# A GRU with eight experts: the experts' and the candidate's products as quarters of 32 stationary columns, and the low half of y on GpSimd

## What is computed

```python
# x [16, 256, 512], h0 = cond_2048 [16, 512]
def cell(h, x):
    gi = x @ W_ih + b_ih                  # [16, 1536]
    gh = h @ W_hh + b_hh
    i_r, i_z, i_n = jnp.split(gi, 3, axis=-1)
    h_r, h_z, h_n = jnp.split(gh, 3, axis=-1)
    r = sigmoid(i_r + h_r); z = sigmoid(i_z + h_z)
    n = tanh(i_n + r * h_n)
    h_new = (1.0 - z) * n + z * h
    return (h_new, h_new)
hs = swapaxes(scan(cell, h0, swapaxes(x, 0, 1)), 0, 1)          # [16, 256, 512]
s = hs.reshape(-1, 512)
logits = s / max(norm(s), 1e-12) @ router_w                     # 8 experts
rw, selected = top_k(softmax(logits), 2); rw = rw / sum(rw)
out = 0
for e in range(8):
    out = out + combine[:, e, None] * (s @ Wa[e] @ Wb[e])       # 512 -> 128 -> 512
return x + out
```

## Time and profile before

| what | value |
|---|---|
| median of 3 runs | 1091.35 us (1091.34 to 1095.48) |
| the profiled execution's own time | 1092.62 us |
| its span, first to last instruction | 1090.7 us |
| mean granted clock of TensorE | 0.995 of full speed |
| busy: PE, DVE, ACT, POOL | 96%, 83%, 60%, 15% of the span |
| matmuls, weight loads | 28880, 28880 |
| chain that ended last, by engine | PE 88%, DVE 6%, ACT 2%, DMA 2% |

### The profile page before, as it was taken

The page is one execution under the profiler, slowest core; times in us unless marked ns, Lnnn a source line. Parts: engine busy times, 40 slices in busy tenths (PEclk is TensorE's granted clock), DMA queues, the critical chain, the costliest instruction groups (busy, mean ns, idle before and its releaser), DMA issues.

```text
span 1090.7 us, 66722 instructions
## 1 busy us (share of the span) xinstructions
PE 1042.4 (96%) x28880; PEld 846.9 (78%) x28880; DVE 907.2 (83%) x3475; ACT 657.6 (60%) x2445; POOL 163.9 (15%) x419
## 2 busy tenths in 40 slices
PE   2679999999999999999999999999999999999996
PEld 2567788888888888888888888888888888888874
DVE  5689888888888888888888888888888888888885
ACT  4576666666665666566666666566666666665552
POOL 3011211111111111111111111111111111110111
PEclk9899999999999999999999999999999999999999
DMA  9801011111101121101112110101111110110000
GB/s 235 202 14 23 24 33 21 26 34 33 32 24 25 22 33 32 33 24 33 23 23 33 33 33 23 30 18 32 34 32 28 28 23 23 33 24 14 14 14 21
DMA packets 48037, 39.23 MB, mean 36 GB/s; under 512 B 33296, under 2 KB 37504, under 8 KB 47744
## 3 DMA queue, kind: packets, MB, share of 16 engines
q1 hardware_dynamic: 47168, 31.81, 13.3%
q10 hardware_dynamic: 576, 3.15, 0.9%
HBM read 18.95 MB, written 8.39 MB: 25 GB/s over the span
## 4 chain that ended last, share of the span: by engine, by line
PE 88%; DVE 6%; ACT 2%; DMA 2%; issue 1%; SPq 1%; POOL 0%; POOLq 0%; DVEq 0%; ACTq 0%
PE ybank L904 17%; PE pairs L819 15%; PE obank L923 14%; PE gates L851 10%; PE gates L856 10%; PE nbank L837 7%; PE zbank L862 5%; PE zbank L866 5%; PE pairs L812 3%; DMA whh<-in_L_cond_W_hh 2%; PE nbank L880 1%; PE nbank L886 1%; DVE tr L692 1%; DVE acc L744 1%; SPq L315 1%
## 5 line engine op out<-in xcount | busy, mean ns | idle before, releaser
L819 PE MATMUL pairs<-wx,xs 128*32 128x256 f16 x6144 | 214.8, 275 | 0.0
L904 PE MATMUL ybank<-hparts,wa 128*128 128x128 f16 x3000 | 210.7, 220 | 2.8 <-DVE y L732 1.9
L819 PEld LDWEIGHTS pairs<-wx,xs 128*32 128x32 f16 x6144 | 153.2, 97 | 61.5 <-issue 50.9
L923 PE MATMUL obank<-wb,y 128*128 128x512 f16 x741 | 200.2, 379 | 0.3 <-DVE acc L744 0.3
L524 ACT ACTIVATE rr<-pre 128x64 f32<-128x64 f32 x256 | 65.7, 256 | 217.8 <-DVE pre L695 217.8
L904 PEld LDWEIGHTS ybank<-hparts,wa 128*128 128x128 f16 x3000 | 168.3, 98 | 30.4 <-DVE y L732 3.7
L851 PE MATMUL gates<-whh,st 128*32 128x256 f16 x4096 | 157.2, 274 | 16.5 <-DVE st L718 12.7
L856 PE MATMUL gates<-whh,hparts 128*32 128x256 f16 x4096 | 157.0, 273 | 0.0
L692 DVE STREAM_TRANSPOSE tr<-gates 128x256 f32<-128x256 f32 x256 | 115.1, 449 | 43.3 <-PE gates L856 30.5
L744 DVE SCALAR_TENSOR_TENSOR acc<-obank,comb,acc 128x512 f32<-128x512 f32 x186 | 138.5, 744 | 1.5 <-PE obank L923 1.5
L837 PE MATMUL nbank<-xs,win 128*128 128x128 f16 x1512 | 126.1, 220 | 2.8 <-ACT gi_n L514 2.8
(11 more groups left out here) (122 smaller groups left out, 1558.8 us busy)
## 6 DMA issues: line engine op xcount, KB each, us to landing
xin<-in_x SPq DMA_DIRECT2D x32, 256.0 KB
out<-outb SPq DMA_DIRECT2D x32, 256.0 KB
wih<-in_L_cond_W_ih ACTq DMA_DIRECT2D x4, 768.0 KB, 9.2
whh<-in_L_cond_W_hh SPq DMA_DIRECT2D x16, 192.0 KB, 13.1
wih<-in_L_ffn_Wb SPq DMA_DIRECT2D x1, 2048.0 KB, 12.4
wih<-in_L_ffn_Wa SPq DMA_DIRECT2D x8, 128.0 KB, 8.2
whh<-in_L_ffn_Wa SPq DMA_DIRECT2D x8, 128.0 KB, 6.3
xs<-xh SPq DMA_TRANSPOSE x58, 2.5
```

The source lines that it names most:

```text
L819: mm = nc.tensor.matmul(bank[32 * j:32 * j + 32, P:3 * P], turned(b, k, ph)[:, t0:t0 + 2 * B], wx[:, pw, k, j, :], start=False, stop=(k == ...
L904: mm = nc.tensor.matmul(y_at(m)[:, 0:P], wa[:, pw, k, e, :], hparts[:, f % HB, k, :, ph * B:(ph + 1) * B], start=(n == 0), stop=(n == 3 * ...
L923: mm = nc.tensor.matmul(o_at(m)[:, :], y[:, m % 2, ph, :], wb[:, pw, m % NE, :], start=(n == 0), stop=(n == 2))
```

## The change

Three products are written as quarters. For each j = 0 to 3 the columns 32j to 32j + 32 of the stationary operand (`wa`, `win` or `y`) are multiplied by the same moving columns as before, and the output goes to partitions 32j to 32j + 32 of the same bank. One matmul becomes four, one weight load four: 12 become 48 in `expert_down`, 6 become 24 in half of `n_part`, 3 become 12 in `expert_up`. `route` keeps its 128 stationary columns.

VectorE's `split_y` is taken out. ScalarE's `split_y` has a second activation that copies `ybank` as float32 into a new tile `y32`, and GpSimd's new `low_y(m)` subtracts the high part of `y` from it. `expert_down` waits for `yhi_ready` and `y32_ready` in place of `ylo_ready`; `expert_up` still waits for `ylo_ready`.

GpSimd's list is interleaved by steps: `split_x` goes in two halves (s = 7 and s = 0 of the next block), `add_squares` in two pieces (`fold_squares` at s = 1, `add_squares` at s = 2), each held until step n's `both_parts_ready`, and each ahead of that step's `low_y`.

```diff
@@ gpsimd
+            def split_x(b, half, n):
+                of = slice(half * D // 2, (half + 1) * D // 2)
                 pool.wait_ge(xhi_ready, b + 1)
                 pool.wait_ge(x_scaled, b - 2)
+                pool.wait_ge(both_parts_ready, 2 * (n + 2))
+                low = nc.gpsimd.tensor_tensor(xh[:, b % 2, 1, of], x128[:, of], xh[:, b % 2, 0, of], ALU.subtract)
...
+            def low_y(m):
+                pool.wait_ge(yhi_ready, m + 1)
+                pool.wait_ge(y32_ready, m + 1)
+                wait(pool, o_done, m - 1)
+                nc.gpsimd.tensor_tensor(y[:, m % 2, 1, :], y32[:, :], y[:, m % 2, 0, :], ALU.subtract
+                                        ).then_inc(ylo_ready, 1)
...
+            def beside(n):
+                i, s = n // S, n % S
+                if s == 1 and 1 <= i:
+                    fold_squares(i - 1, n)
+                if s == 2 and 1 <= i:
+                    add_squares(i - 1, n)
+                if s == X_AT + 1 and i + 3 < NB:
+                    split_x(i + 3, 0, n)
+                if s == 0 and 1 <= i and i + 2 < NB:
+                    split_x(i + 2, 1, n)
+                if 0 <= n - DOWN:
+                    low_y(n - DOWN)
+                if s == 3 and 1 <= i:
+                    invert_norm(i - 1)
+                    gaps(i - 1)
+                if s == 4 and 1 <= i:
+                    combine(i - 1)
@@ scalar, split_y
                 nc.scalar.activation(y[:, m % 2, 0, :], y_at(m)[:, 0:P], ACT.Copy, scale=1 / PART_SCALE
                                      ).then_inc(yhi_ready, 1)
+
+                wait(act, ylo_ready, m)
+                nc.scalar.activation(y32[:, :], y_at(m)[:, 0:P], ACT.Copy, scale=1 / PART_SCALE).then_inc(y32_ready, 1)
@@ vector
-            def split_y(m):
-                dve.wait_ge(yhi_ready, m + 1)
-                nc.vector.scalar_tensor_tensor(out=y[:, m % 2, 1, :], in0=y_at(m)[:, 0:P], scalar=1 / PART_SCALE,
-                                               in1=y[:, m % 2, 0, :], op0=ALU.mult, op1=ALU.subtract
-                                               ).then_inc(ylo_ready, 1)
@@ tensor, n_part
-                    mm = nc.tensor.matmul(n_at(b, m)[:, 0:P], win[:, pw, k, m, :], turned(b, k, ph),
-                                          start=(i == 0), stop=(i == 11), skip_group_check=True)
+                    for j in range(K):
+                        own = slice(32 * j, 32 * j + 32)
+                        mm = nc.tensor.matmul(n_at(b, m)[own, 0:P], win[:, pw, k, m, own], turned(b, k, ph),
+                                              start=(i == 0), stop=(i == 11), skip_group_check=True)
@@ tensor, expert_down
-                wait(pe, ylo_ready, m if m <= LAST else m - 1)
+                wait(pe, yhi_ready, m if m <= LAST else m - 1)
+                wait(pe, y32_ready, m if m <= LAST else m - 1)
...
-                        mm = nc.tensor.matmul(y_at(m)[:, 0:P], wa[:, pw, k, e, :],
-                                              hparts[:, f % HB, k, :, ph * B:(ph + 1) * B],
-                                              start=(n == 0), stop=(n == 3 * K - 1))
+                        for j in range(K):
+                            own = slice(32 * j, 32 * j + 32)
+                            mm = nc.tensor.matmul(y_at(m)[own, 0:P], wa[:, pw, k, e, own],
+                                                  hparts[:, f % HB, k, :, ph * B:(ph + 1) * B],
+                                                  start=(n == 0), stop=(n == 3 * K - 1), skip_group_check=True)
@@ tensor, expert_up
-                    mm = nc.tensor.matmul(o_at(m)[:, :], y[:, m % 2, ph, :], wb[:, pw, m % NE, :],
-                                          start=(n == 0), stop=(n == 2))
+                    for j in range(K):
+                        own = slice(32 * j, 32 * j + 32)
+                        mm = nc.tensor.matmul(o_at(m)[own, :], y[:, m % 2, ph, own], wb[:, pw, m % NE, :],
+                                              start=(n == 0), stop=(n == 2), skip_group_check=True)
```

More of the change, by code:

```diff
@@ L135, in gru_moe_kernel @@
         comb = sb("comb", [P, NE])
+        y32 = sb("y32", [P, P])
         y = sb("y", [P, 2, 2, P], F16)
@@ L220, in gru_moe_kernel @@
         yhi_ready = sem("yhi_ready")
+        y32_ready = sem("y32_ready")
         ylo_ready = sem("ylo_ready")
@@ L395, in split_win, with fold_squares, add_squares @@
                                         ).then_inc(win_split, 1)
-            def split_x(b):
+            def split_x(b, half, n):
+                of = slice(half * D // 2, (half + 1) * D // 2)
                 pool.wait_ge(xhi_ready, b + 1)
                 pool.wait_ge(x_scaled, b - 2)
[L401 to L405, removed]
+                pool.wait_ge(both_parts_ready, 2 * (n + 2))
+                low = nc.gpsimd.tensor_tensor(xh[:, b % 2, 1, of], x128[:, of], xh[:, b % 2, 0, of], ALU.subtract)
+                if half:
+                    low.then_inc(xlo_ready, 1)
+            def fold_squares(f, n):
                 pool.wait_ge(sq_ready, f + 1)
-                if f + 1 < NB:
-                    pool.wait_ge(both_parts_ready, 2 * ((f + 1) * S + 3))
+                if n < T:
+                    pool.wait_ge(both_parts_ready, 2 * (n + 2))
                 nc.gpsimd.tensor_tensor(sq2[:, :], sq[:, 0:2 * P], sq[:, 2 * P:4 * P], ALU.add).then_inc(sq_step, 1)
+            def add_squares(f, n):
                 pool.wait_ge(sq_step, f * SQ_STEPS + 1)
                 wait(pool, logits_done, f)
+                if n < T:
+                    pool.wait_ge(both_parts_ready, 2 * (n + 2))
                 nc.gpsimd.tensor_tensor(sqs[:, :], sq2[:, 0:P], sq2[:, P:2 * P], ALU.add).then_inc(sq_step, 1)
+            def low_y(m):
[4 more added lines that the diff above has]
+                                        ).then_inc(ylo_ready, 1)
             def invert_norm(f):
@@ L447, in _, with last_experts @@
                 split_win(k)
[L448 to L456, removed]
+            def beside(n):
[15 more added lines that the diff above has]
+                    combine(i - 1)
+            def last_experts():
+                fold_squares(NB - 1, T)
+                add_squares(NB - 1, T)
+                for m in range(LAST, T):
+                    low_y(m)
+                    if m == LAST + 3:
+                        invert_norm(NB - 1)
+                        gaps(NB - 1)
+                    if m == LAST + 4:
+                        combine(NB - 1)
+            for n in range(T):
+                beside(n)
+            last_experts()
         @block.scalar
@@ L752, in beside @@
                     add_expert(n - ADD)
-                if 0 <= n - DOWN < T:
-                    split_y(n - DOWN)
                 if s == 3 and 1 <= i <= NB:
@@ L763, in last_experts @@
                 for m in range(LAST, T):
-                    split_y(m)
                     add_expert(m - 1)
```

## The result

The changed kernel takes 1411.65 us (median of 4 runs, 1406.27 to 1416.30) against 1092.02 (median of 4, 1091.34 to 1095.48). The ratio is 1.292, with a 95% interval of 1.286 to 1.297. The prediction was 1052, in a range of 1046 to 1076: wrong in sign, by 360 us. The profiled execution took 1410.65 us, with a span of 1408.4 and a mean granted clock of 0.994, so TensorE's clock is the same as before.

What follows compares the result with a forecast made beforehand. TensorE, busy 96% of the span, was taken as the bound. Gains of 38.1 us in steps 24 to 247 and 2.3 in steps 12 to 23, 40.4 together, took 1092.6 to about 1052 us, range 1046 to 1076.

Steps and rivals of the forecast that it cites:

- Columns: TensorE's three products: four quarters cost what one full product did, gain or loss under 0.02 us a step, taken as nothing.
- The two boundaries: TensorE ahead of `ybank` and L812, where stationary width changes between 32 and 128: 0.11 + 0.09 = 0.20 us a step gained.
- Steps: Odd steps from 4.00 to 3.80 us, even from 3.85 to 3.71; a block gains 1.36, 28 blocks 38.1 us.
- the floor of 3.71: The recurrence loop from `st` through gates, transposes, sigmoid and tanh to `st` holds any step at 3.71 us, whatever TensorE does.
- VectorE, ScalarE, GpSimd: Other engines in full blocks: VectorE's dropped `y`, ScalarE's extra copy and GpSimd's subtractions, each taken as costing or gaining nothing.
- The 2.3 us of steps 12 to 23: Gain where VectorE bounds: 0.21 us in each of about eight steps, 0.14 to 0.20 in the rest.
- likeliest case: The 1052 us forecast with its allowances for GpSimd's overlap, ScalarE and a longer loop: 1047 to 1064 us, 73%.
- the third rival: TensorE cannot issue the quarters fast enough, slower above 22.6 ns a pair; 1273 us at 27 ns; 8%.
- The price of 27 ns: Pace of the 256-column quarters on TensorE, used as cost per pair: a step of 4.7 us, 1273 us in all.
- collide: GpSimd's `low_y` meets VectorE's `pre` in every step: loop of 3.85 us, about 1073 us; 12%.
- boundaries do not go: TensorE's 0.20 us a step stays or comes back: steps of 4.00 and 3.85 us, 1090 us; 4%.
- What would show it: Checks for the profile after: steps of 3.80 and 3.71, no 0.1 gaps; wrong if quarters or `pre` slow, or TensorE waits for `y`.

Runs made afterwards that it cites:

- e7_s3: Kernel before with ScalarE's `y32` copy, GpSimd's `low_y` and interleaved list, and quarters in all three products at s = 3 of each block only: 1094.04 us, ratio 1.0009.
- e5_one_term: Changed kernel with only the first of three TERMS in the three quartered products, 28 quarters a step in place of 84: 1046.56 us, ratio 0.958.
- e8_halves: Changed kernel with halves of 64 stationary columns in place of quarters of 32 in all three products: 1123.37 us, ratio 1.028.
- e1_y_way: Kernel before with only ScalarE's `y32` copy, GpSimd's `low_y` and GpSimd's interleaved list, the three products full: 1092.56 us, ratio 0.9992.

## Why the prediction was wrong, point by point

*Columns* (a four of quarters costs what a full product did): right for the array, and only for it. The sum had nothing for the 63 pairs more in a step; that is the term that failed, below. `ybank` 0.67, `nbank` 0.34, `obank` 0.65 in stretches without a stop, in the changed kernel and in e7_s3.

*The two boundaries*: right. 0.11 + 0.09 predicted, 0.22 measured in e7_s3's step s = 3, and e5_one_term shows both gone. By the page "TensorEngine Tiling (Array Packing)" of the Trainium skill, Key Properties, a change of tiling mode drains TensorE. The trace agrees, and e8_halves from a second side: 64 columns beside 32 lose 0.11 and 0.09 too.

*Steps*: right as far as work goes (3.79 and 3.63 without the stops for 3.80 and 3.65), and the floor of 3.71 stands in e5_one_term. But a step of 172 to 176 pairs doesn't fit into a block of 127, and the 224 steady steps take 5.34 us on the mean; two of them took 3.73. A block of eight steps takes 42.7 us on the mean where 30.8 was predicted. Only the steps 4 to 12, which have no experts' products but the first, take 3.71 to 3.80; steps 13 and 14 take 5.68 and 5.54.

*VectorE, ScalarE, GpSimd*: what was taken at nothing is nothing. e1_y_way is within 0.1% of before. In the changed kernel `low_y` has a median of 0.43 (0.46 predicted), `pre` one of 0.29 and at most 0.34, so the two don't collide, and next to nothing waits for `low_y`. The two views, of L426 and L737 (min, median, max in ns):

```profile
L426 POOL TENSOR_TENSOR y<-y x256: 421/428/960, 89.7 to 1401.6; 128x128 f16<-128x128 f32 x128
```

```profile
L737 DVE TENSOR_TENSOR pre<-tr x256: 291/292/341, 38.6 to 1377.9; 128x128 f32<-128x128 f32 x128
```

The 2.3 us of steps 12 to 23, most of them from VectorE's `y`, are not shown in the time: e1_y_way's interval goes from 2.2 us less to 0.3 more than before. In the two profiles these steps take 50.0 us before and 48.8 in e1_y_way, so there are signs of 1.2. The upper end of the likeliest case, 1064, leaves 5 us for GpSimd's overlap once 4 and 3 are taken, where the bound of 0.25 in three steps of eight comes to 28 x 3 x 0.25 = 21; `pre` shows that nothing of it was needed.

*The step that failed* is the one that set aside the third rival, "TensorE cannot issue the quarters fast enough", and so put the 63 pairs more in a step at nothing in the sum. The rival had the right sign and the right break-even, 3.93 / 174 = 22.6 ns for a pair, and 8%. What went wrong is the argument against it and the price. The argument was a run of 76 pairs at 17 ns each. That run is shorter than a block of 127 pairs: it shows how fast instructions that are already there are issued, not how fast new ones come. The only pace that the trace of before showed over more than a block was its own, 35 ns, so between 35 and 22.6 ns it held nothing that spoke for the change. Measured: 3.97 us for 127 pairs, 31 ns. The price of 27 ns was that of the moving columns in the earlier trace rows, a matter of the array and not of the supply; with 31 ns a step of 174 pairs is 5.4 us, and 1092 + 236 x (5.4 - 3.93) = 1439, near the 1412 that came. Even the rival's own price was 139 us short. The mechanism was not named either: the row of the instruction queue stood on the page of before and was not read. It gives 1090.7 / 229 = 4.76 us for a block on the mean, against 2.72 that the change would ask for.

*The rivals "collide" and "boundaries do not go"* did not come about. "What would show it" had no row for this: it looked for slow quarters and for waits on y, and the loss is in neither.

## What to carry to other kernels

Count the instructions, not only the columns: divide an engine's instructions by the span, and before a change that multiplies them ask whether the trace shows the pace that it needs held over more than one block of 256. A burst proves nothing for a sustained pace; "issue" idle that falls on every line alike, 256 instructions apart, is the mark of it. In this kernel, splitting a matmul into quarters was free on the array and gained where it took away a change of stationary width. What ate the gain were the stops, and in these runs they were all but absent only where pairs of matmul and weight load were asked for no faster than one in some 33 ns (4.23 us for 127), in each stretch of a few microseconds and not only on the mean.

## What the runs showed of the hardware

- TensorE's instructions came in blocks of 256 (16.4 KB), one in 3.97 to 4.05 us where they were the bound: 15.5 ns an instruction, 31 ns a pair of weight load and matmul. With 4.23 us a block asked for there was one stop in 28 groups of eight steps, with 3.80 there was one in nearly all of them.
- In the changed kernel the packet of the next block began 1.3 us behind TensorE's restart, took 1.1, and TensorE restarted 1.4 behind its end (medians of 254 stops): 3.8 us together.
- About one block was stored ahead: a single step of 190 pairs among steps of 111 stopped, or let the next step stop, in 20 of 28 cases, by up to 0.8 us.
- A change between 32 and 64 stationary columns lost as much as one between 32 and 128: 0.11 and 0.09 us.
- 64 matmuls of 32 stationary columns and one moving column, each with a weight load, took 0.62 us with the boundary behind them, some 8 ns each: some four times faster than the 31 ns at which pairs were supplied.
- Four quarters read the same moving operand, laid out in pieces of 16 elements, at no cost: 48 took 0.67 us, where 12 full products had taken 0.68.
